# Every other one of the first twelve input blocks issued from ScalarE's queue instead of SyncE's

## What is computed

```
g = group_norm(x)                       # 32 groups of 16 channels, over 16 x 32 x 48 values
def step(prev, g_w):                    # Wc is 512 x 512, from conv_w[:, :, 0, 4]
    y = einsum('oc,nch->noh', Wc, prev) + conv_b[None, :, None]
    y = where(y >= 0, y, prelu_a * y)
    return y + g_w
fl  = scan of step over w = 1..47, started with g[..., 0]
out = scan of step over w = 46..0 of fl, started with fl[..., 47]
return x + out
```

## Time and profile before

| what | value |
|---|---|
| time, median of 3 runs | 378.8 us (378.78 to 379.49) |
| the profiled execution | 379.27 us, its span 377.5 us |
| granted TensorE clock | 0.998 |
| busy in the span | PE 94%, DVE 76%, ACT 60%, POOL 6% |
| HBM read | 13.63 MB, all in the first 36 us |
| first step's last quarter starts (L264) | 38.96 us |

### The profile page before, as it was taken

How to read it: one execution, slowest core, us unless ns; L and a number is a source line. 1 busy time by engine, 2 the same in 40 slices (tenths; PEclk the granted TensorE clock), 3 DMA queues, 4 the chain that set the end, 5 groups by cost and what they waited for, 6 DMA issues and landing times.

```text
span 377.5 us, 10144 instructions
## 1 busy us (share of the span) xinstructions
PE 354.2 (94%) x3116; PEld 352.3 (93%) x3116; DVE 285.4 (76%) x920; ACT 226.6 (60%) x798; POOL 24.0 (6%) x36
## 2 busy tenths in 40 slices
PE   0269999999999999999999999999999999999996
PEld 0169999999999999999999999999999999999996
DVE  2677888888878888656656778778787787787786
ACT  4754465565665665655655656656656556566564
POOL 2178200000000000000000000000000000000002
PEclk9999999999999999999999999999999999999999
DMA  7998000000000000000000112212212112122123
GB/s 304 421 414 306 3 0 0 1 0 0 1 0 0 0 1 0 0 0 0 0 0 0 58 56 83 83 56 83 82 57 83 71 68 83 60 79 83 56 83 111
DMA packets 10665, 26.30 MB, mean 70 GB/s; under 512 B 1313, under 2 KB 1569, under 8 KB 10657
## 3 DMA queue, kind: packets, MB, share of 16 engines
q1 hardware_dynamic: 10512, 26.22, 17.9%
q10 hardware_dynamic: 144, 0.00, 0.0%
HBM read 13.63 MB, written 12.58 MB: 69 GB/s over the span
## 4 chain that ended last, share of the span: by engine, by line
PE 90%; DMA 4%; POOL 2%; SPq 1%; ACT 1%; issue 1%; DVE 1%; ACTq 0%; DVEq 0%; POOLq 0%
PE psum L294 88%; DMA xin<-in_x 4%; PE psum L254 1%; SPq L206 1%; PE psum L264 1%; POOL state L518 1%; POOL state L515 1%; POOL rstd L508 0%; PE psum L247 0%; ACT state L315 0%; DVE state L382 0%; ACT above L352 0%; DVE state L430 0%; ACT state L318 0%; ACT dev L325 0%
## 5 line engine op out<-in xcount | busy, mean ns | idle before, releaser
L294 PE MATMUL psum<-state,w_t 128*128 (+1 forms) x2976 | 332.8, 275 | 0.0
L294 PEld LDWEIGHTS psum<-state,w_t 128*128 128x128 f32 x2976 | 332.5, 192 | 0.3 <-DVE state L430 0.2
L352 ACT ACTIVATE above<-psum,params 128x128 f32<-128x128 f32 x376 | 139.7, 372 | 132.4 <-PE psum L294 129.2
L425 DVE TENSOR_TENSOR state<-above,state 128x128 f32 (+1 forms) x376 | 109.4, 291 | 69.5 <-ACT above L352 58.4
L354 ACT ACTIVATE below<-psum,negative 128x128 f32<-128x128 f32 x376 | 139.8, 372 | 0.0
L430 DVE SCALAR_TENSOR_TENSOR state<-below,negative,state 128x128 f32 (+1 forms) x376 | 123.5, 349 | 6.7
L468 DVE TENSOR_TENSOR state<-state,xin (+1 forms) x47 | 32.1, 684 | 0.0
L364 DVE BATCH_NORM_STATS2 bstat<-xin 128x6 f32<-128x512 f32 x34 | 21.5, 674 | 11.9 <-DMA xin<-in_x 11.9
L382 DVE TENSOR_SCALAR state<-xin,mean,rstd 128x320 f32<-128x320 f32 (+1 forms) x68 | 26.7, 438 | 0.3 <-POOL rstd L508 0.3
L538 POOL TENSOR_TENSOR state<-state,xin 128x128 f32<-128x128 f32 x4 | 2.3, 573 | 330.0 <-DVE state L430 330.0
L236 PE MATMUL psum<-chan,same_group 128*128 128x128 f32 (+1 forms) x8 | 2.3, 381 | 17.8 <-DVE chan L378 17.8
(11 more groups left out here) (31 smaller groups left out, 27.4 us busy)
## 6 DMA issues: line engine op xcount, KB each, us to landing
out_y<-state SPq DMA_DIRECT2D x47, 256.0 KB, 2.0
xin<-in_x SPq DMA_DIRECT2D x13, 768.0 KB, 12.6
xin<-in_x SPq DMA_DIRECT2D x5, 256.0 KB, 18.3
xin<-in_x SPq DMA_DIRECT2D x2, 512.0 KB, 19.4
w_t<-in_w SPq DMA_DIRECT2D x4, 256.0 KB, 11.2
out_y<-state SPq DMA_DIRECT2D x1, 192.0 KB, 1.9
out_y<-state SPq DMA_DIRECT2D x1, 64.0 KB, 1.6
params<-in_par ACTq DMA_DIRECT2D x1, 2.5 KB, 4.9
```

The lines of the kernel that those rows point to most:

```text
L294: mm = nc.tensor.matmul(psum[:, 4 * par + o, 0:COLS], w_t[:, k, o * P:(o + 1) * P], xs[k], start=k == 0, stop=k == 3)
L352: nc.scalar.activation(above[:, par, o, :], z, ACT.Relu, bias=params[:, o:o + 1], scale=1.0).then_inc(above_done, 1)
L425: nc.vector.tensor_tensor(sts[o], above[:, par, o, :], sts[o], ALU.add).then_inc(part_done, 1)
```

## The change

The loads of blocks 1, 3, 5, 7, 9 and 11 are issued by ScalarE, behind its load of params and ahead of everything else in its program. SP issues the other ten blocks (14 transfers) in order, then w. No size, destination or semaphore is changed.

```diff
+ACT_QUEUE = range(1, 12, 2)
...
         @block.sync
         def _(sp):
-            for b in range(NBLK):
+            for b in (b for b in range(NBLK) if b not in ACT_QUEUE):
                 w0 = 0
                 for i, size in enumerate(pieces(b)):
                     sp.dma_start(xin[:, b // N, b % N, w0:w0 + size, :],
...
         @block.scalar
         def _(act):
             act.dma_start(params[:, :], par[:, :]).then_inc(params_loaded, 16)
+            for b in ACT_QUEUE:
+                act.dma_start(xin[:, b // N, b % N, :, :], x[b // N, b % N]).then_inc(x_loaded[b][0], 16)
             act.wait_ge(counts_set, 4)
```

## The result

The changed kernel takes 380.87 us (median of 5 runs, 380.68 to 380.97), the one before in its five runs of the same comparison 378.95: a ratio of 1.0044, interval 1.0033 to 1.0056. By the medians that is +1.9 us where +1.5 was forecast. The profiled execution takes 380.68 us with a span of 378.7; by the two profiled executions the change costs 1.4 us.

What follows compares the result with a forecast made beforehand. TensorE's chained steps bound the kernel, so only the lead-in could move their start. Odd blocks 1.88 us late, less slack, start the steps 1.5 us later: median 380.3 us, own range 379.7 to 380.9, 8-in-10 range 378.7 to 381.1.

Steps and rivals of the forecast that it cites:

- own range: Median time expected if the main forecast holds: 379.7 to 380.9 us, chance 0.60.
- rival 1: Lead-in: SP's lead is not a full block; with no lead even blocks land 1.88 us late, +1.9, 380.7; chance 0.13.
- Order of landing: Lead-in transfers: queues alternate row by row; even blocks land on time, odd ones one block late, +1.88 us each.
- Rival 2: Lead-in transfers: served in the order of issue, so landings stay as before, 378.8 us; chance 0.14.
- rival 3: Lead-in transfers: two queues lift the rate, leaving +0.5 or so (379.3) or no change; chance 0.09, of which 0.04 faster.
- rival 4: ScalarE in the lead-in: its own slow issues hold it until 12 us, +3.3, 382.1; chance 0.04.
- Group 1 and 2: Lead-in: ScalarE reads group 1's deviations 0.96 us later; TensorE is free for group 2's means 1.0 us later.
- Last groups: End of lead-in: VectorE's last channel work shifts 1.88 - 0.21 = 1.67 us; GpSimd's last rstd starts 1.5 us later.
- From profile to median: Whole kernel: 380.8 us by the profiled execution's own time, less 0.5 for the runs' median, gives 380.3.

## Why the prediction was right, and what was off

- *How near it was*: the median of 380.87 lies just inside the own range, 0.03 us under its upper end, and rival 1's 380.7 is nearer to it than 380.3. The number alone could not tell the two apart; the landings do. That the median is no farther off is in part luck, since the last three points below don't go the same way: -0.4, +0.7 and +0.2 us.
- *Order of landing*: right in every block shown (the odd ones 1.84 to 1.98 us late, block 4 0.34 early), and the experiments show the reason that it gave: turns by rows, and a lead that hangs on params. Rival 2 (order of issue) falls by the landings. Rival 1's order appears once params are taken out. The arbitration by whole packets of 9 to 17 descriptors, as the Trainium skill has it (DMA: Bandwidth & Descriptors, Queues, rings and completion order), would have had block 4 1.88 us early; it was 0.34.
- *Rate (rival 3)*: (28.12 - 20.72) / 4 = 1.85 us a block from block 7 to 11, against 1.88: nothing that matters.
- *Issues (rival 4)*: over at 4.78, 4.4 forecast; hidden behind block 0.
- *Group 1 and 2*: deviations at 24.25 (24.1), TensorE free at 30.25 (30.4), means used at 30.32 (30.4). Two errors hide in this. keep_up(9, 0) starts 1.11 us later and not 0.96, and takes 5.18 us instead of the 5.67 that the sum kept. And it is VectorE that decides when group 2 starts, not TensorE as the sum has it: with keep_up(9, 0) at 4.28 us it starts no sooner.
- *Last groups, the term that was mis-sized*: var_eps ready at 37.67, not 38.08, so the last rstd +1.10 and not +1.5 by the profiled pair. Block 11 is 1.84 us late instead of 1.88, and I took off 0.21 for VectorE's idle where 0.55 went: from block 11 to group 3's last channel work VectorE takes 34.35 - 26.28 = 8.07 us before and 35.64 - 28.12 = 7.52 after. Before, the end of this stretch reads

```profile
31.47 1.23 DVE L364 BATCH_NORM_STATS2 bstat<-xin 128x6 f32<-128x512 f32 x2
32.75 0.22 DVE L378 BATCH_NORM_AGGREGATE chan<-bstat 128x2 f32<-128x15 f32 x1
32.88 1.25 DVE L364 BATCH_NORM_STATS2 bstat<-xin 128x6 f32<-128x512 f32 x2
```

The two starts of channel work come 1.28 and 1.47 us behind those of the statistics before them, where after it is 1.14 for both (33.24 to 34.38, 34.50 to 35.64). These 0.47 us I read as waits for ScalarE, of which the profile names 0.21; ScalarE was late behind a keep_up(9, 0) of 5.67 us. The other 0.1 is in the statistics of blocks 12 and 13, and its cause is open. TensorE, forecast to be free at 35.6 and to wait, is free only at 35.87 and level with VectorE.
- *From profile to median*: the sum was made against an execution in which TensorE's way had already cost the kernel before some tenths. Its median execution is 378.95, not 379.27, and the changed kernel's stays at VectorE's floor, its median 0.19 above its profiled execution. What is lost is therefore more by the medians (1.9) than by the profiled pair (1.4); subtracting the 0.5 us between profile and median from both kernels alike was wrong, by 0.7 us.
- *Outside the span*: 1.96 to 2.02 us in the five runs of the changed kernel, 1.69 to 1.80 in the runs of the one before. These 0.2 us were in no step: the sum put them at nothing. With six small loads they stay at 1.71 to 1.80 and with one block in three pieces at 1.77; with blocks 1, 3 and 5 moved they are 1.73 to 1.93, and with the five up to 9 they change from run to run (1.69 to 2.20). So it is not the number of issues; what it is the profile doesn't show, and it stays open.

## What to carry to other kernels

Where transfers already fill the DMA engines, as here at 422 GB/s and a share of 1.02, don't expect rate from a second queue; it changed only who lands when. The two queues took turns row by row while both had work, so each transfer took twice as long and the one that was next in line paid. Move a load to another queue only if it may come late, and look at what stands at the head of each queue, however small. Before adding a delay to a profiled execution, find out which of two nearly level ways set its end, and whether that one is the same in each execution.

## What the runs showed of the hardware

- A small packet (a row of 20 B, and one in nine for the semaphore) takes a turn of some 26 ns on its engine beside rows of 6144 B that take 0.235 us (1.88 us for 8). 144 packets of params cost every block about 0.2 us by the same count (an estimate: 9 turns of 26 ns).
- The same 16 products of keep_up(9, 0) took 5.67 to 6.37 us in three executions of the kernel before and 4.51 and 5.18 in two of the changed one. Over all twelve profiles with 16 products they split by what TensorE did just before. Where it waited 0.60 to 1.98 us for ScalarE's deviations of group 1, they took 5.60 to 6.37 us (seven profiles). Where it went on without a wait, they took 4.51 to 5.18 (five). The change is of the second kind. Whether the wait is the cause was not tried by itself. TensorE's windows of L254 in the profile of before (length, busy PE, busy PEld, granted clock, DMA share, GB/s) show 6 records in one microsecond and 11 in the next, with the granted clock at 1.00 in both; what sets the moment is open:

```profile
27.00:28.00 1.00, 1.00 (x6) 1.00 (x6) 1.00 1.02 391
28.00:29.00 1.00, 1.00 (x11) 1.00 (x10) 1.00 1.05 416
```
